# Routing of tokens to experts: a pipeline of eight unrolled groups, and the expert weights split later

## What is computed

```
logits  = layernorm(x) @ Wg.T                    # 8 experts
routing = sigmoid(logits); scores = routing + bias
top2    = top_k(scores, 2); weights = routing[top2] / sum
h1, h3  = x @ W1[e].T, x @ W3[e].T               # x: the normalised row, e: a chosen expert
out     = x_residual + sum over e: weight_e * (silu(h1) * h3) @ W2[e].T
```

## Time and profile before

| | us |
|---|---|
| median of 3 runs | 3019.73 |
| lowest to highest | 3019.2 to 3022.58 |
| the profiled execution | 3024.8 |
| its span | 3023.3 |
| PE busy in the span | 2648.8 (88%) |
| mean granted clock of PE | 0.947 |

### The profile page before, as it was taken

How to read it: one execution, slowest core, us unless ns; L and a number is a source line. 1 busy time by engine, 2 the same in 40 slices (tenths; PEclk the granted TensorE clock), 3 DMA queues, 4 the chain that set the end, 5 groups by cost and what they waited for, 6 DMA issues and landing times. The chain is left out here.

```text
span 3023.3 us, 49992 instructions
## 1 busy us (share of the span) xinstructions
PE 2648.8 (88%) x15042; PEld 1814.2 (60%) x15043; DVE 1931.0 (64%) x3971; ACT 1352.9 (45%) x2725; POOL 1040.0 (34%) x1209
## 2 busy tenths in 40 slices
PE   7999999999999999995788889888888434299997
PEld 6888888888888888884333333333333111166665
DVE  6555566656555666554888878888888278444443
ACT  4333444444333444432477766776666322022221
POOL 2111122211111222213355565566555346432322
PEclk9999999999999999997899999999999666599999
DMA  3110011122110111103666777777776264455554
GB/s 112 42 42 28 13 42 42 42 84 70 43 42 0 42 42 42 42 28 88 113 121 135 140 128 130 133 137 131 132 138 114 54 230 158 157 98 104 98 104 77
DMA packets 140545, 265.50 MB, mean 88 GB/s; under 512 B 39217, under 2 KB 42161, under 8 KB 138945
## 3 DMA queue, kind: packets, MB, share of 16 engines
q1 hardware_dynamic: 111376, 195.58, 29.1%
q0 software_dynamic: 24496, 60.72, 9.7%
q10 hardware_dynamic: 4608, 8.39, 0.8%
HBM read 139.43 MB, written 64.90 MB: 68 GB/s over the span
## 5 line engine op out<-in xcount | busy, mean ns | idle before, releaser
L1420 DVE TENSOR_REDUCE b_negmax<-b_ps_s 128x2 f32<-128x1024 f32 x512 | 616.8, 1221 | 117.6 <-PE b_ps_s L1563 114.2
L1292 ACT ACTIVATE b_probs<-b_ps_s 128x1024 f32<-128x1024 f32 x512 | 517.1, 1022 | 258.3 <-PE b_ps_s L1574 257.2
L260 POOL TENSOR_SCALAR probs<-probs,rinv 128x256 f32<-128x256 f32 x256 | 242.2, 946 | 1099.7 <-DVE rinv L412 1099.7
L294 ACT ACTIVATE probs<-ps_s,negmax 128x128 f32<-128x128 f32 x256 | 94.2, 368 | 480.6 <-DVE negmax L405 480.6
L1563 PE MATMUL b_ps_s<-b_stack 54*128 54x512 f32 x1024 | 228.8, 444 | 80.0 <-ACT b_probs L1292 50.1
L1574 PE MATMUL b_ps_s<-b_stack 56*128 56x512 f32 x1024 | 255.1, 496 | 49.4 <-DVE b_negmax L1420 30.8
L1574 PEld LDWEIGHTS b_ps_s<-b_stack 56*128 56x128 f32 x1024 | 97.9, 189 | 333.6 <-issue 183.9
L1585 PE MATMUL b_ps_o<-b_probs,b_v_stack 128*32 128x512 f32 x2048 | 283.6, 627 | 5.2 <-ACT b_probs L1292 5.2
L516 PE MATMUL ps_proj<-xT_h,wq_h 128*128 128x512 f32 x512 | 215.6, 421 | 0.0
L2181 POOL DMA_INDIRECT out<-e_y,e_place_int x71 | 110.8, 1560 | 277.1 <-DVE e_y L2244 174.7
L516 PE MATMUL ps_proj<-xT_h,wq_l 128*128 128x512 f32 x512 | 201.2, 393 | 0.0
(11 more groups left out here) (299 smaller groups left out, 6730.1 us busy)
## 6 DMA issues: line engine op xcount, KB each, us to landing
b_stack<-b_split SPq DMA_DIRECT2D x240, 128.0 KB
e_row<-rows_by_expert SPq DMA_DIRECT2D x71, 258.0 KB, 3.2
x_in<-in_x SPq DMA_DIRECT2D x16, 1024.0 KB, 7.5
b_out_tiles<-row_sum_inverses SPq DMA_DIRECT2D x64, 256.0 KB
x<-acc SPq DMA_DIRECT2D x15, 1024.0 KB, 5.1
b_stack<-b_late SPq DMA_DIRECT2D x96, 128.0 KB
acc<-in_x SPq DMA_DIRECT2D x8, 1024.0 KB, 6.0
acc<-x SPq DMA_DIRECT2D x8, 1024.0 KB, 5.7
```

The source lines that it names most:

```text
L260: nc.gpsimd.tensor_scalar(probs[:, s, P:3 * P], probs[:, s, P:3 * P], rinv[:, s, 1:2], None, ALU.mult).then_inc(probs_done, 1)
L294: nc.scalar.activation(probs[:, s, 0:P], ps_s[s][:, 0:P], ACT.Exp, bias=negmax[:, s, 0:1], accum_out=rowsum[:, s, 0:1])
L1292: nc.scalar.activation(probs[:, k % 2, p, :, :], ps[:], ACT.Exp, scale=0.25).then_inc(e_done, 1)
L1420: nc.vector.tensor_reduce(negmax[:, k, p, :], ps[:], AX.X, ALU.max, negate=True).then_inc(m_reduced, 1)
```

## The change

The routing block is written out as eight single groups, in an order of its own on each engine.

- Rows are normalised by ACT (`apply`, one ACTIVATE with scale and bias for 128 rows, in place); POOL computes 1/sqrt and the bias (`shifts`, four small instructions). DVE only takes the statistics.
- There are six slots for row groups instead of three, two transposed buffers `xT` instead of one, and eight `place_int`. Groups 0 to 5 are loaded at once, 6 and 7 when groups 0 and 1 have been sent.
- PE transposes group G+1 and counts group G-1 before the logits of group G.
- POOL splits no weights. The raw weights of experts 0 to 3 are loaded by SP in this block. Only experts 0 and 1 are split in it (ACT, and DVE at its end). Experts 2 to 7 are split in the first eight tiles of `run_experts`, by ACT (`weights_high(u + 2)`) and DVE (`weights_low(u + 1)`); ACT's queue loads 4 to 7 there, straight into the buffer of the low parts. Those eight tiles are unrolled on PE, ACT and DVE.
- Padding is written by SP and ACT, four plain transfers each at an address read from `pad_row_int`. The block no longer waits for `w2`; PE does before its first down product.

The core of the diff:

```
+                def apply(G):
+                    act.wait_ge(shift_done, G + 1)
+                    for n in range(TB):
+                        nc.scalar.activation(group_rows(G)[:, n, 0:H], group_rows(G)[:, n, 0:H], ACT.Identity,
+                                             bias=shift[:, G, n:n + 1], scale=rstd[:, G, n:n + 1]).then_inc(xn_done, 1)
...
+                for G in range(2, 6):
+                    shifts(G)
+                send(0)
+                send(1)
+                send(2)
+                shifts(6)
+                send(3)
+                shifts(7)
+                for G in range(4, GROUPS):
+                    send(G)
...
+                row_stats(0)
+                row_stats(1)
                 dve.wait_ge(wg_high, 1)
...
+                row_stats(2)
+                row_stats(3)
+                lows(0)
+                constants()
+                row_stats(4)
+                row_stats(5)
+                lows(1)
+                for G in range(GROUPS):
+                    choose(G)
+                    place_rows(G)
+                    if G + 2 < GROUPS:
+                        lows(G + 2)
+                    if G in STATS_AT:
+                        row_stats(STATS_AT[G])
...
+                for e in range(SPLIT_FIRST):
+                    weights_low(e)
+                dve.wait_ge(w13_split[1], SPLIT_FIRST)
...
+                for G in range(1, GROUPS):
+                    if G + 1 < GROUPS:
+                        transposes(G + 1)
+                    count(G - 1)
+                    logits(G)
+                    logits_rows(G)
+                count(GROUPS - 1)
...
                     nc.scalar.activation(gate[:], ps_h[i][:, 0:FF], ACT.Silu).then_inc(gate_done, 1)
+                    if isinstance(u, int) and SPLIT_FIRST <= u + 2 < E:
+                        weights_high(u + 2)
+                    if isinstance(u, int) and RAW_FIRST <= u + 2 < E - 2:
+                        load_weights(u + 4)
...
                         meta(u + 1, t + i, 1 - i)
+                    if isinstance(u, int) and SPLIT_FIRST <= u + 1 < E:
+                        weights_low(u + 1)
...
+                    if isinstance(u, int) and SPLIT_FIRST <= u < E:
+                        pe.wait_ge(w13_split[1], u + 1)
                     pe.wait_ge(x_low, u + 1)
```

More of the change, by code:

```diff
@@ L1830, in _ @@
             def _(sp):
[L1832 to L1838, removed]
@@ new lines, in _ @@
+                for e in range(RAW_FIRST):
+                    raw = w13_raw[:, e] if e < SPLIT_FIRST else w13[1][:, e].bitcast(F32)
+                    sp.dma_start(raw, w_13T[e].rearrange("(k p) f -> p k f", p=P)).then_inc(w13_loaded, 16)
+                for G in (6, 7):
+                    sp.wait_ge(scattered[SLOTS[G]], 16 * 2 * TB)
+                    load(G)
+                sp.wait_ge(numbers, 7)
+                sp.dma_start(rows[PAD_ROW:PAD_ROW + P], pad_rows[:]).then_inc(padded[0], 16)
@@ L1889, in group @@
-                def group(G, t, i):
-                    first, last = isinstance(G, int) and G == 0, isinstance(G, int) and G == GROUPS - 1
-                    if not first:
-                        send(G - 1, (i + 2) % 3, range(TB // 2))
-                    if not last:
-                        rstd_of(G + 1)
-                    if not first:
-                        send(G - 1, (i + 2) % 3, range(TB // 2, TB))
-                        wait_alone(pool, w13_high, G, (consts, 11))
-                        e = expert(G - 1)
-                        nc.gpsimd.tensor_tensor(w13[1][:, e], w13_raw[:, e], w13[0][:, e].bitcast(F32),
-                                                ALU.subtract).then_inc(w13_low, 1)
@@ L2103, in group @@
                     ins.then_inc(counted, 1)
-                pe.wait_ge(consts, 11)
-                transposes(0, 0)
-                pe.wait_ge(wg_low, 1)
-                in_groups(pe, GROUPS, group)
-def run_experts(nc, rows, out, w13, w2, ident, tile_expert, tile_expert_int, tile_row_int, sent_before,
+                pe.wait_ge(consts, 9)
+                transposes(0)
+                pe.wait_ge(wg_low, 1)
+                logits(0)
+                transposes(1)
+                logits_rows(0)
@@ L2153, in run_experts @@
         gT_done = sem("gT_done")
+        w13_loaded = [sem(f"w13_loaded{n}") for n in range(2)]
         y_filled = sem("y_filled")
@@ L2262, in _ @@
                 meta(0, 0, 0)
-                in_steps(dve, TILES, tile, first=4, last=3)
+                in_steps(dve, TILES, tile, first=E, last=3)
                 y_copy(TILES - 1, (TILES - 1) // 2, (TILES - 1) % 2)
@@ L2325, in _ @@
                 transposes(0, 0, 0)
-                in_steps(pe, TILES, tile, last=3)
+                in_steps(pe, TILES, tile, first=E, last=3)
                 g_transposes(TILES - 1)
```

325 lines of the change are left out of this document (181 added, 144 removed).

## The result

| | before | changed |
|---|---|---|
| median of the runs | 3019.47 us (3016.93 to 3022.58, 4 runs) | 2989.26 us (2980.51 to 2996.58, 4 runs) |
| ratio, 95% interval | 1 | 0.9892 (0.9872 to 0.9913) |
| profiled run, its span | 3024.8, 3023.3 us | 2994.48, 2993.0 us |
| granted clock, mean | see the earlier trace rows for the stage | 0.957 |

The kernel is 30 us (1.1%) faster, and the time lies in the range, 9 us above the 2980 forecast. I cut each span at three places that every profile has: SP's first load of the routing block (2415.14 before, where ACT's loads start too), PE's first transpose of tile 0 (2630.25 before), and the transposes of `g` of tile 8, the first tile that needs no fresh weights; before, they stand 51.8 us behind PE's first transpose.

What follows compares the result with a forecast made beforehand. POOL's sends were taken as the new limit of the routing block, where DVE had set the pace. First tile 74.8 us earlier, 34.7 given back in the tiles: -40.1 from 3019.73, so 2980 us; range 2960 to 3001.

Steps and rivals of the forecast that it cites:

- Start of the sends: Opening of the routing block: first load lands in 5.8 us, first send at 2453.4, 0.9 us after placing.
- 64 sends at 1.34 us: POOL in the routing block: each send 1.049 us plus 0.29 of issue, 85.9 us in all.
- the second split's 2.3: End of DVE's routing work: the second of two weight splits stretches POOL's sends, adding 2.3 us.
- POOL is the limit: Routing block: POOL's sends need 10.7 us a group, more than DVE's 8.8 and the PE loop's 10.2.
- the loop through PE: Routing block, second limit: ranking, count, logits, copy, transposes and exponential take 10.2 us a group, 7.9 at 2.4 GHz.
- the charge of nothing: ACT's row scaling in the routing block: 2.2 us a group, hidden in ACT's idle time, so no cost.
- Padding "hides behind the sends, ends near 2541": End of the routing block: padding on SP and ACT hides behind POOL's sends; without that cover 3 to 8 us.
- Barrier and first rows, 9.9 us, "unchanged": Between the routing block's end and the first tile: 9.9 us as before, first tile starting at 2555.5.
- Stalls in the tiles: Before six tiles PE idles 4.1 us each, waiting for DVE's weight split: 24.5 us given back.
- rival "splits do hide": Tiles: the weight splits run beside PE's work and cost nothing, giving 2945 us; chance 0.04.
- rival with starved sends: Routing block: DVE keeps POOL from writing descriptors; at 1.26 us more a send, 3060 us; chance 0.07.
- other two rivals of the clock: Six tiles: clock stays high over the waits, 2969 us, chance 0.17; or 1.2 GHz throughout, 3001 us, 0.12.

Runs made afterwards that it cites:

- e0: The changed kernel run again without any edit: 2981.27 us, ratio 0.9868 to the kernel before.
- e7: Changed kernel with the splits of experts 0 and 1 moved from DVE's end to POOL, behind the sends of groups 4 and 5: 2986.42 us, ratio 0.9878.
- e5: Changed kernel with the edits of e1 and e4 together: 2943.11 us, ratio 0.9732.
- e4: Changed kernel with 3 MB of `w2` issued behind SP's padding, still in the routing block: 2977.20 us, ratio 0.9839.
- e3: Changed kernel with `w2` of experts 2 to 7 (3 MB) loaded in the tiles, not in the routing block: 2986.07 us, ratio 0.9885.
- e6: Changed kernel with the padding back on POOL, as 8 indirect transfers behind the last send: 2984.44 us, ratio 0.9873.
- e8: e5 with 3 MB of `w2` taken out of the routing block, loaded in pairs behind the row loads of tiles 1, 3 and 5: 2952.28 us, ratio 0.9765.
- e2: Changed kernel with 16 useless matmuls ahead of PE's wait for the split in tiles 2 to 7: 2967.16 us, ratio 0.9820.
- e1: Changed kernel with DVE splitting the weights of tile u+2, not u+1, in its tile u: 2955.41 us, ratio 0.9767.

## Why the forecast held, and where it was off

- **Start of the sends.** Forecast 38.3 us after the block's start, measured 37.6. The first load's 5.8 was 5.65. The lag between placing and send was 0.3 and not 0.9. Right.
- **64 sends at 1.34 us.** The mean of 1.049 was the mis-sized term. It is 0.97 in the first profile, 1.02 in e0 with DVE's two splits under them, 0.98 in e7 with none. The prediction read one stretched send in the rows; the trace of before has six more, one in each turn of a body of the loop, under the row scaling that the change takes from DVE:

```profile
2481.49 1.41 POOL L1886 DMA_INDIRECT rows_by_expert<-r_xn,r_place_int  x1 [0.20 <-issue]
```

So I kept a mean with stretches by work that the change removes, 6 x 0.45 us, and then added the second split's 2.3 on top; both splits together cost 2.4. From first send to last end it is 91.4 us, of which 6.5 are stalls, and 88.2 in e5, against 92.2.
- **POOL is the limit.** Right, but narrowly: DVE's placings in e5 are 10.4 us apart in the mean (2445.64 to 2518.19, seven periods), nearer to the 10.2 estimated for the loop through PE than to the 8.8 of DVE's own work (whose terms add to 8.7). The single periods go from 8.6 to 12.4, so that the loop sets them is not shown. POOL's group is 11.0. ACT's row scaling takes 2.9 us for a group in e0 against the 2.2 taken, and the charge of nothing held.
- **Padding "hides behind the sends, ends near 2541".** Wrong. On SP it landed after 19.4 us, behind `w2`: in e0 134.1 us after the block's start, where 126 was forecast and POOL's last send ended at 125.6. SP is ready 0.4 us before POOL's drain ends there, and e4, without this delay, gains nothing. In the first profile, where `w2` was issued 8 us later than in e0, it ends the block, 1.8 us behind POOL's drain.
- **Barrier and first rows, 9.9 us, "unchanged".** This is the step that failed: 16.4 in the first profile, 12.9 in e0. Before, `w2` was issued at 2585.75 and landed in 15.6 us, 18 ahead of POOL's last issue. With a block shorter by 70 us the same 4 MB run beside the last sends, and the landing of the last eight takes 8.5 us instead of the 5.9 of e3. e3 (9.1), e6 (9.9) and e8 (10.4) have the bytes elsewhere, and about the drain of before. I had charged the sharing to the padding alone.
- **The two errors cancel.** In e0 the sends are 4.8 us cheaper (125.6 against 130.4) and the drain 3.0 dearer; routing 138.5 against 140.4. The first profile adds 7 us, to 145.4: 3.4 before the last send's end and 3.5 in the drain, where `w2`, late by the stalls, holds POOL's drain 1.7 us longer and then SP's padding 1.8.
- **Stalls in the tiles.** 24.5 forecast, 23.2 as PE's own waits and 24.4 in e2. Clock 10.2 forecast, 11 by the difference to e2. Right, and right for the reason given: the semaphores order the split between two tiles (e1). The rival "splits do hide" would have needed one tile more of lead, which e1 gave.
- **The rival with starved sends** is out: DVE's ranking and placing beside every send left them at 0.98 (e7). The other two rivals of the clock are out by the stretches around the wait: it falls, and it comes back within the tile.
- **The 9 us.** In the profiled execution they are 9.8: 7 from the stalls less 2 by which e0's routing is under the forecast, 3.3 of later start of the block, in phases that nobody touched, and 1.4 in the tiles and the rest. The nine runs of the changed kernel in two sessions have a median of 2984.03 us. The range held mostly because the clock's bounds made it wide; it had no term for either of these.

## What to carry to other kernels

When an edit shortens a block, look at what used to be finished long before its end, above all large loads on other queues: here 4 MB came to lie beside the last transfers and made the barrier 3 us dearer, wherever they stood in the queue. When work is moved into a software pipeline, follow the semaphores for the tile that it is due in: one tile of lead was worth 33 of the 36 us, and a short idle time of PE costs half as much again in clock. Terms of a few microseconds are read between two fixed instructions of the program, in several profiles; the span alone moved by more for no reason of the change.

## What the runs showed of the hardware that I had not expected

- The clock stays high through an idle time of 3.9 us and falls as the work resumes: 1.00 idle, 0.67 and 0.50 in the four microseconds behind, 0.97 in the next two. 16 matmuls without use in that time keep it at 1.00 and save 11 us in six tiles.
- Indirect sends land in 2.8 to 3.1 us at the median in the middle of the block (e0 and e4), in 5.9 beside the padding (e3) and in 8.1 to 8.5 beside padding and 3 to 4 MB of `w2` (e0, e1, e2, e4, e5), though those go on another queue.
- A DVE instruction of 0.2 to 0.4 us that meets POOL's tensor_tensor of 4.5 us lasts until that ends, in nine of nine cases (4.12 to 5.40 us, eight tensor_scalars and one tensor_tensor); an indirect send under DVE's tensor_tensor of 2.3 us is stretched by 0.9 to 1.9, one under four tensor_scalars of 128x512 by 0.45.
- Two sessions of one kernel on one chip differ by 11.7 us (0.4%) in the median, with stalls of 3 to 6 us on ACT, DVE and PE in the profile of one and none in that of the other. An interval from one session doesn't hold this.
